# A gated cross-attention layer with a routed low-rank feed-forward: where the attention output is normalised and added to x

## The reference, cut to what matters

```python
# attention: LayerNorm(x) gives q, ctx gives k and v; dim = 128, 8 heads of 64
qh = softmax(Wq q, axis=-2) * 64 ** -0.5        # over the 64 of a head
kh = softmax(Wk k, axis=-1)                     # over the 1024 columns
context = einsum('bhdn,bhen->bhde', kh, vh)
out = Wo (context . qh) + bo                    # 128 x 1024 per sequence
norm = max(sqrt(sum(out * out, axis=1)), 1e-12) # one number per column
x = x + tanh(g_xattn) * out / norm * g * sqrt(128)
# feed-forward on rows of LayerNorm(x): 64 experts of rank 16, the best 16 are gated
scores = xf @ Wr.T;  gates = softmax(top16(scores))
h = xf A  (1024 x 1024);  out = (h * gates) B * 2
x = x + tanh(g_ffn) * out
```

## Time and profile before

| | us |
|---|---|
| median of 3 runs | 1103.09 |
| lowest, highest | 1101.88, 1105.66 |
| the profiled execution: span | 1101.1 |
| its own time | not given beside the span |
| stage one, from the first instruction to the last matmul of L823 | about 650 |
| stage two | about 450 |
| PE, DVE, ACT, POOL busy | 1046.2, 702.1, 510.1, 419.3 |

### The profile page before, as it was taken

One profiled execution on the slowest core, in us unless ns is written; L12 is line 12 of the kernel. 1 busy time (PEld: TensorE's weight loads), 2 busy tenths in 40 slices (PEclk: granted clock), 3 DMA queues, 4 the chain that ended last, 5 costly groups with the idle time before them and its releaser, 6 DMA issues. The chain is left out here.

```text
span 1101.1 us, 17249 instructions
## 1 busy us (share of the span) xinstructions
PE 1046.2 (95%) x5732; PEld 880.6 (80%) x5732; DVE 702.1 (64%) x1522; ACT 510.1 (46%) x855; POOL 419.3 (38%) x294
## 2 busy tenths in 40 slices
PE   6899999999999999999999879999999999999997
PEld 4688888888888888888788767888888888888886
DVE  6887887878788787878877648444434443334321
ACT  5576568558656755856675535311112221111110
POOL 2656657655655765575566411000000110000000
PEclk9999999999999999999999978999999999999999
DMA  6002012201201210220110038111111111111000
GB/s 225 24 20 77 30 46 76 76 13 63 76 19 57 76 63 13 76 76 19 57 57 34 6 139 235 39 39 38 38 38 38 38 38 38 38 38 38 19 22 36
DMA packets 25705, 60.34 MB, mean 55 GB/s; under 512 B 2448, under 2 KB 12176, under 8 KB 25680
## 3 DMA queue, kind: packets, MB, share of 16 engines
q1 hardware_dynamic: 23376, 58.99, 15.5%
q10 hardware_dynamic: 2304, 1.05, 0.3%
HBM read 43.26 MB, written 16.78 MB: 55 GB/s over the span
## 5 line engine op out<-in xcount | busy, mean ns | idle before, releaser
L1079 POOL TENSOR_TENSOR yT_lo<-yf,yT_hi 128x512 fp32r<-128x512 f32 x32 | 40.8, 1296 | 354.8 <-ACT yT_hi L1236 354.8
L266 POOL TENSOR_TENSOR qe<-qe,qrec 128x1024 f32<-128x1024 f32 x64 | 121.2, 1905 | 96.5 <-DVE qrec L542 96.5
L547 DVE TENSOR_TENSOR qT_lo<-ps,qT_hi 128x512 fp32r<-128x512 f32 x128 | 82.5, 686 | 47.6 <-ACT qT_hi L384 47.2
L259 POOL TENSOR_TENSOR qhalf<-qe 128x512 f32<-128x512 f32 x64 | 82.1, 1283 | 72.4 <-ACT qe L377 72.4
L1226 ACT ACTIVATE yf<-ps 128x512 f32<-128x512 f32 x32 | 17.5, 595 | 189.4 <-PE ps L1119 189.4
L67 PE MATMUL ps<-aT_hi,yT_hi 128*128 128x512 f32 x256 | 103.0, 402 | 0.0
L67 PE MATMUL ps<-bT_hi,hT_hi 128*128 128x512 f32 x256 | 102.6, 401 | 0.0
L68 PE MATMUL ps<-bT_hi,hT_lo 128*128 128x512 f32 x256 | 101.2, 395 | 0.0
L69 PE MATMUL ps<-bT_lo,hT_hi 128*128 128x512 f32 x256 | 101.2, 395 | 0.0
L69 PE MATMUL ps<-aT_lo,yT_hi 128*128 128x512 f32 x256 | 101.1, 395 | 0.0
L68 PE MATMUL ps<-aT_hi,yT_lo 128*128 128x512 f32 x256 | 101.1, 395 | 0.0
(11 more groups left out here) (159 smaller groups left out, 2628.3 us busy)
## 6 DMA issues: line engine op xcount, KB each, us to landing
ctx_in<-in_ctx SPq DMA_DIRECT2D x16, 512.0 KB, 3.3
x_in<-in_x SPq DMA_DIRECT2D x16, 512.0 KB, 3.2
x_res<-in_x SPq DMA_DIRECT2D x16, 512.0 KB, 3.7
x_scratch<-x SPq DMA_DIRECT2D x16, 512.0 KB, 2.9
out<-b_stage SPq DMA_DIRECT2D x16, 512.0 KB, 2.9
stage<-in_L_ffn_A SPq DMA_DIRECT2D x8, 512.0 KB, 4.6
stage<-in_L_ffn_B SPq DMA_DIRECT2D x8, 512.0 KB, 6.8
stage<-x_scratch SPq DMA_DIRECT2D x8, 512.0 KB, 3.9
```

Source lines behind the costliest of these rows:

```text
L259: nc.gpsimd.tensor_tensor(qhalf[:, p % 2, :].rearrange("p (h d) -> p h d", d=DH // 2), v[:, :, 0:DH // 2], v[:, :, DH // 2:DH], ALU.add).t ...
L266: nc.gpsimd.tensor_tensor(v, v, w, ALU.mult).then_inc(q_norm, 1)
L547: nc.vector.tensor_tensor(qT[1][:, :, v], psT[:, h, :].rearrange("p (j n) -> p j n", n=P), qT[0][:, :, v].bitcast(f32), ALU.subtract).then ...
```

## The change

Three parts, and what follows from them.

1. Stage one no longer makes x2. `spread_norms`, the copies to `usb`, `gated`, `finish`, `finish_last` and the load of `x_res` go. SP stores `osb` to a scratch `u_dram` after `out_o`, and the 8 columns of norms to `rn_dram`, word by word, so that there they stand in the order of the 1024 columns.
2. Stage two loads x, u and the norms (one row of 4 KB, broadcast to 128 partitions). GpSimd multiplies and adds (`residual`), and VectorE's `stats` waits for that (`x2_done`). u has two buffers, which the normalised `y` uses too, so SP loads u of b + 2 once y of b is transposed. Weight rows are loaded behind the first two sequences' loads.
3. The root's start is one step in place of two: y = MAGIC - s / 2 on the integers, a SCALAR_TENSOR_TENSOR with a constant tensor `magic`. VectorE does `roots` behind `sum_q` and `max_q(b, 0)`.

```diff
@@ rsqrt_step
         if k == 0:
-            last = nc.vector.tensor_scalar(t.bitcast(i32), s.bitcast(i32), 1, None, ALU.logical_shift_right)
-        elif k == 1:
-            last = nc.vector.tensor_scalar(y.bitcast(i32), t.bitcast(i32), -1.0, float(MAGIC), ALU.mult, ALU.add)
-        elif k % 3 == 2:
+            last = nc.vector.scalar_tensor_tensor(y.bitcast(i32), s.bitcast(i32), -0.5, magic[:, 0:s.shape[1]],
+                                                  ALU.mult, ALU.add)
+        elif k % 3 == 1:
             last = nc.vector.tensor_tensor(t, y, s, ALU.mult)
...
@@ stage one, SP
                     if late:
-                        wait_apart(sp, sp_turns, (x2_done, b - 1))
-                        sp.dma_start(x2_dram[bass.ds(b - 2, 1)].rearrange("o p n -> (o p) n"),
-                                     x2[:, :]).then_inc(x2_stored, 16)
-                        if tail:
-                            load(x_res[:, :], x, b - 1, xres_loaded)
+                        wait_apart(sp, sp_turns, (root_step, NCH * (b + 2)))
+                        with nc.allow_non_contiguous_dma(reason="one norm to a word, in the order of the columns"):
+                            sp.dma_start(rn_dram[bass.ds(b - 2, 1)].rearrange("o (k p) -> p (o k)", p=P),
+                                         root_y[:, 0:BK]).then_inc(rn_stored, 16)
+                    if tail:
+                        wait_apart(sp, sp_turns, (o_out, 2 * b))
+                        sp.dma_start(u_dram[bass.ds(b - 1, 1)].rearrange("o p n -> (o p) n"),
+                                     osb[:, :]).then_inc(u_stored, 16)
@@ stage one, GpSimd
-                    if late and tail:
-                        gated(b - 2, 0)
-                        gated(b - 2, 1)
...
-                    if late and tail:
-                        finish(b - 2)
@@ stage one, VectorE
                     if ahead:
                         stats(b + 1)
-                    if late or ahead:
-                        roots(b + 1, b - 2 if late else None, b + 1 if ahead else None)
-                    if late and not tail:
-                        finish_last(b - 2)
                     if tail:
                         sum_q(b - 1, 2)
                         sum_q(b - 1, 3)
                     if head and started(b):
                         max_q(b, 0)
+                    if late or ahead:
+                        roots(b + 1, b - 2 if late else None, b + 1 if ahead else None)
...
+                    if late and tail:
+                        dve.wait_ge(rn_stored, 16 * (b - 1))
@@ stage one, TensorE
-                    if late:
-                        spread_norms(b - 2, next(turn))
@@ stage two, SP
+            def load_attention(b, half):
+                sp.dma_start(u_in[:, half, :],
+                             u_dram[bass.ds(b, 1)].rearrange("o p n -> (o p) n")).then_inc(u_loaded[half], 16)
+                sp.dma_start(rn_in[:, half, :], rn_dram[bass.ds(b, 1)].broadcast_to([P, D])).then_inc(rn_loaded[half], 16)
+
+            sp.wait_ge(u_stored, 16 * NB)
+            sp.wait_ge(rn_stored, 16 * NB)
+            for b in range(2):
+                load(b, b)
+                load_attention(b, b)
             for t in range(NSTG + early, 2 * KC):
                 load_weight_rows(sp, t, A, B, stage, st_loaded, b_ready, w_T)
...
             def group(i, last):
                 for j in range(SLOTS):
                     b = SLOTS * i + j
+                    if not last or j < 2:
+                        sp.wait_ge(y_T, 2 * b + 2)
+                        load_attention(b + 2, j % 2)
                     sp.wait_ge(res_done, 2 * b + 2)
                     sp.dma_start(out[bass.ds(b, 1)].rearrange("o p n -> (o p) n"),
                                  res[:, j % 2, :]).then_inc(out_stored[j % 2], 16)
                     if not last:
                         load(b + SLOTS, j)       # now x, before x2
@@ stage two, GpSimd: residual(0), residual(1), then in pass b residual(b + 2) ahead of lo_y(b + 1)
+            def residual(b, j, i):
+
+                slot, half, uses = j % SLOTS, j % 2, i + j // SLOTS
+                pool.wait_ge(u_loaded[half], 16 * (2 * i + j // 2 + 1))
+                pool.wait_ge(rn_loaded[half], 16 * (2 * i + j // 2 + 1))
+                nc.gpsimd.tensor_tensor(rn_in[:, half, :], u_in[:, half, :], rn_in[:, half, :],
+                                        ALU.mult).then_inc(u_done, 1)
+                pool.wait_ge(x_loaded[slot], 16 * (uses + 1))
+                pool.wait_ge(u_done, b + 1)
+                nc.gpsimd.tensor_tensor(x2b[slot], rn_in[:, half, :], x2b[slot], ALU.add).then_inc(x2_done, 1)
@@ stage two, VectorE, first step of stats
-                    dve.wait_ge(x2_loaded[slot], 16 * (uses + 1))
+                    dve.wait_ge(x2_done, b + 1)
```

More of the change, by code:

```diff
@@ L85, in flamingo_layer @@
         w_T = osem("w2_T")
[L86 to L89, removed]
+        u_stored, rn_stored = osem("u_stored"), osem("rn_stored")
         ps = outer.enter_context(nc.psum_tensor("ps", [P, 8, 512], f32))
@@ L416, in body @@
                         hi_xn(b, 1)
-                    if late and tail:
-                        for h in range(2):
-                            act.wait_ge(rn_mm, 2 * b - 4 + h + 1)
-                            nc.scalar.activation(usb[:, 512 * h:512 * h + 512], psT[:, h, :],
-                                                 ACT.Copy).then_inc(rn_out, 1)
                     if tail:
@@ L511, in roots @@
                     for k in range(NCH):
-                        if k == 1 and var is not None and started(var):
+                        if k == 0 and var is not None and started(var):
                             dve.wait_ge(xn_done, var)
@@ L813, in square_norms @@
                     last.then_inc(ss_mm, 1)
-                def spread_norms(b, before):
-                    pe.wait_ge(root_step, NCH * (b + 4))
-                    for h in range(2):
-                        free_T(before, h)
-                        for n in range(4):
-                            dst = psT[:, h, n * P:n * P + P]
-                            col = 4 * h + n
-                            last = nc.tensor.matmul(dst, root_y[:, col:col + 1].broadcast_to([P, P]), ident[:, :],
-                                                    start=True, stop=True)
-                        last.then_inc(rn_mm, 1)
                 def early_weights():
@@ L943, in load_weight_rows, with ffn_phase @@
                      ).then_inc(st_loaded[t % slots], 16)
-def ffn_phase(nc, ident, gates, ps, stage, st_loaded, w_T, early, x2_stored, x2_first, x2_loaded, started, wait_apart, rsqrt_step,
-              three_pass, A, B, Wr, x2_dram, out):
+def ffn_phase(nc, ident, gates, ps, stage, st_loaded, w_T, early, u_stored, rn_stored, started, wait_apart, rsqrt_step,
+              three_pass, x, A, B, Wr, u_dram, rn_dram, out):
     f32 = mybir.dt.float32
@@ L962, in ffn_phase @@
     LN_EPS = 1e-5
[L963 removed]
+    NEWTON, NCH = 3, 10
     NEG = -3.0e38
@@ L1015, in ffn_phase @@
         f_mm, res_done = sem("f_mm"), sem("res_done")
+        x_loaded = [sem(f"x2_loaded{n}") for n in range(SLOTS)]
+        u_loaded = [sem(f"u_loaded{n}") for n in range(2)]
+        rn_loaded = [sem(f"rn_loaded{n}") for n in range(2)]
+        u_done, x2_done = sem("u_done"), sem("x2_done")
         psH, psF, psY, psG, psS = ps[:, 0:2, :], ps[:, 2:4, :], ps[:, 4:6, :], ps[:, 6, :], ps[:, 7, 0:E]
@@ L1085, in _ @@
             lo_y(0)
-            with pool.Fori(1, NB) as b:
-                lo_y(b)
+            for j in range(SLOTS):
+                body(0, j, True)
+            with pool.Fori(1, NB // SLOTS - 1) as i:
+                for j in range(SLOTS):
+                    body(i, j, True)
+            for j in range(SLOTS):
+                body(NB // SLOTS - 1, j, j < 2)
         @block.tensor
```

104 lines of the change are left out of this document (42 added, 62 removed).

## The result

The changed kernel takes 1160.57 us (median of 4 runs, 1157.83 to 1162.71), the kernel before 1102.49 us on the same chip (1100.51 to 1105.66). The ratio is 1.0524, 95% interval 1.0504 to 1.0544. The profiled execution took 1160.09 us, with a span of 1158.0 us: 56.9 us more than before.

The account below looks back on a forecast made before the run. TensorE, busy 95% of the span, was taken as the bound, its largest wait being `spread_norms` for the roots. The span was 1101.1 - 30 + 11 + 45 + 8 = 1135.1 us, so 1137 us measured, range 1108 to 1164.

Parts of the forecast that it names:

- likeliest case: Whole kernel: the prediction's own case, 1137 us with own range 1118 to 1155, chance 0.63.
- Stage one, -30: Stage one: root wait and `spread_norms` matmuls go, later waits return part; 2.25 us per pass gained, bounds -51 and -16.
- `fold`'s wait: Stage one, each pass: TensorE waits about 0.65 us at `fold` because `kc_lo` comes later.
- the hold: Stage one's roots on VectorE: GpSimd's `normalise` holds the second step to +3.63; roots end at +5.3 us after `mm_q(b, 0)`.
- Hand-over, +11: Between the stages: sequence 0's statistics wait for norm store, three loads and two GpSimd instructions; +11 us, bounds +7 and +15.
- Wait of `tr_h(b, 1)`, +45: Stage two's loop: late x2 makes TensorE wait 3.6 us per pass, b = 1 to 13; +45 us, bounds +29 and +64.
- rival A: Stage two: x2's computation is hidden, the change pays only at the hand-over; 1084 or 1063 us, chance 0.10.
- Clock, +8: Stage two: holes make some of `down` run at half speed, 0.6 us per pass; +8 us, bounds 0 and +40.
- Rival B: Stage two: the clock falls in every pass and stays low through most of `down`; 1168 us, chance 0.12.
- Rival C: Hand-over: the store of words takes 20 us in place of 5.5, so +26 there; 1152 us, chance 0.07.
- Rival D: Both stages kinder: stage one gives 47, stage two costs 2.2 us per pass without clock loss; 1094 to 1103, chance 0.08.

Follow-up runs that it names:

- Run 6: Changed kernel with the root's integer start put back to two TENSOR_SCALAR steps: 1173.42 us, ratio 1.0657 to the kernel before.
- run 3: Changed kernel with the norms stored in 128 pieces of 32 bytes, column order not restored: 1154.1 us, ratio 1.0480 to the kernel before.
- run 1: Changed kernel with the stage-two loads of u and norms issued a pass earlier: 1087.99 us, ratio 0.9880 to the kernel before.
- run 5: Changed kernel with stage two's x load issued behind the loads of u and norms: 1147.12 us, ratio 1.0401 to the kernel before.
- Run 2: Changed kernel with 14 unused matmuls on constant data filling the hole before `tr_h(b, 1)`: 1138.09 us, ratio 1.0329 to the kernel before.
- run 8: Changed kernel plus earlier u/norm loads and old roots order (1070.61 us); against that, sequences 0 and 1 load without awaiting the last norms' store: 1069.3 us.
- run 10: Changed kernel plus earlier u/norm loads, old roots order, norms in 128 pieces read permuted, first two sequences' loads not awaiting the last norms' store: 1062.31 us.

## Why the prediction was right, and where its size was off

The direction and the mechanism were right, term by term; 1160.57 lies in the range given (to 1164), above the likeliest case's own (to 1155). Of the 22.9 us by which the span was under-predicted, the clock is 17.9 and the hand-over 4.7.

- **Stage one, -30: right**, -30.25. `fold`'s wait was taken as 0.65 and is 0.64; `output`'s is 0.22 in this pass, where I took 0.75, 0.2 of it by a slip: 8.8 + 1.75 is 10.55, not 10.75. A pass went from 38.8 to 36.6 us, 2.2 less, so some 0.6 us per pass went at places for which I have no row. Two errors cancel, and that the stage came out to the quarter microsecond is luck. The detail of the hold was wrong: I let the first root step pass at a boundary and had the second one held; the first itself is held, and the remaining nine pass. The roots end at the same time either way. The Trainium skill's rule quoted there (SBUF - State Buffer, Who interferes with whom) agrees with the trace, with 1.90 us in place of 0.17. Run 6 adds that an integer step of 9 columns with one SBUF input is held as long, so here two inputs are not needed.
- **Hand-over, +11: mis-sized by the store of words**, 9.9 us to the landing where I took 5.5. From the first load's issue to the third landing it was 6.6 us (628.17 to 634.81) where I had 5.4; GpSimd's two (4.8) and the held root (1.67 in place of 0.16) were as taken. My row for the words was a transfer of 512 KB that landed in 6.8 us, and I went below it because so few bytes are in it. The count of pieces, not the bytes, set the time (run 3: an eighth of the pieces, 4.4 us). The Trainium skill's rule (DMA: Bandwidth & Descriptors, Rules for kernel authors: one descriptor per element) I had put aside as changing no term, which was the wrong conclusion: the packets show it to hold, 14,336 fewer in run 3.
- **Wait of `tr_h(b, 1)`, +45: right**, 45.5, 12 of 3.2 to 4.3 us and the last of 2.0. The point at which rival A would decide was x2 before about 3.6 us earlier; run 1 puts it there, and A's gain appears. Inside the term the x transfer was over-counted and another part under-counted by as much (run 5), so the size has some luck in it; the wait and what it waits for are as forecast.
- **Clock, +8: the term that failed in size**, 25.9, or 2.0 us per pass in place of 0.6. I took a value near the low end "since the work around the hole is dense". Run 2 shows that this density did not protect it: with the holes the clock fell in all 13 passes, without them in none. The row that should have decided was in my own bounds: half of a low stretch of some 6 us, 3.2 us. Three passes cost about that, ten about half of it, so the measured 2.0 lies between the ends but on the upper side. Rival B, the clock low in every pass, was nearer to what happened than my own case, though at 2.0 and not 3 us per pass.
- **Rival C** (words at 20 us) went the right way, by 4.4 of the 14.5 us that it added. **Rival D** did not occur.

## What to carry to other kernels

When a value that was loaded ready-made is now put together from parts, look at what the last part queues behind: here a load issued one iteration sooner turned 5% slower into 1.2% faster with the same work. A hole that a loop adds to TensorE is to be priced twice, once for its length and once for the work behind it at the lower clock; in this kernel 3.5 us of hole cost 2.0 more. Count the pieces of a small store before its bytes, and keep it off the end of a queue in which the next stage's loads stand.

## What the runs showed of the hardware

- The last store of 1024 single words (4 KB) took 9.9 to 11.2 us to land in the seven kernels that wait for it there, 128 pieces of 32 bytes of the same data 4.0 to 4.4 in two. Behind the words, loads that were already issued moved 12 to 37 GB/s for 3 us (run 8); behind the pieces 383 (run 10).
- Idle stretches of TensorE of 1.69 us, one per 39 us pass, left the clock at 2.4 GHz in stage one before. In the changed kernel's stage two all 13 holes, of 3.2 to 4.3 us and one of 2.0, came with a fall to 1.2 GHz within about a microsecond of the return of the work, and it stayed there 3 to 4 us (ten times) or near 7 (three times). In run 5, with holes of 2.6 to 3.5 us, two of 13 (2.57 and 2.80 us) came without it.
- A 9-column VectorE step that met two GpSimd multiplications of 1.88 us each waited for the end of the second, 1.90 us for the step, with one SBUF input (1.91, run 6) as with two. The read of 8 columns from PSUM just ahead of it, beside the first of the two multiplications, took 0.16 us.
- The GpSimd multiplication with one input in steps of 8 words took 2.85 us against 2.34 for 128x1024.
